# Two-of-eight experts: the bf16 division as a logarithm and an exponential, PSUM copies on VectorE, and the expert steps in a new order

## What is computed

```python
scores = jax.nn.sigmoid((xt @ gate.T).astype(jnp.float32))
_, sel = jax.lax.top_k(scores + expert_bias[None, :], TOP_K)      # TOP_K = 2 of 8
...
routed = (routed.astype(jnp.float32) * scores_sorted[:, None]).astype(x.dtype)
xb = routed.astype(jnp.bfloat16)
for e in range(NUM_EXPERTS):
    h = jax.nn.silu(xb @ w1e.T) * (xb @ w3e.T)                    # in bfloat16
    oe = (h @ w2e.T).astype(routed.dtype)
    out_r = out_r + jnp.where((expert_ids == e)[:, None], oe, 0.0)
hs = jax.nn.silu(xt @ shared_w1.T) * (xt @ shared_w3.T)           # in float32
out = hs @ shared_w2.T
out = out.at[token_idx].add(out_r)
```

## Time and profile before

| | us |
|---|---|
| median of three runs | 3227.81 |
| lowest and highest | 3227.55, 3230.34 |
| span of the profiled execution | 3223.9 |
| first statistics of the expert stage start at | 2554.28 |
| last add to x of the expert stage ends at | 2775.66 |

### The profile page before, as it was taken

The page is one execution under the profiler, slowest core; times in us unless marked ns, Lnnn a source line. Parts: engine busy times, 40 slices in busy tenths (PEclk is TensorE's granted clock), DMA queues, the critical chain, the costliest instruction groups (busy, mean ns, idle before and its releaser), DMA issues. The chain is left out here.

```text
span 3223.9 us, 65738 instructions
## 1 busy us (share of the span) xinstructions
PE 2916.0 (90%) x18443; PEld 2458.6 (76%) x18444; DVE 2173.0 (67%) x4391; ACT 2039.8 (63%) x5203; POOL 1594.7 (49%) x2073
## 2 busy tenths in 40 slices
PE   5887999799999999999999999999999966599495
PEld 4665888588888888888888888888888833388463
DVE  7994444476677676677776677676777589766332
ACT  5664666577777776777677677677777456565121
POOL 6993333455555555555555555555555243465201
PEclk9998999899999999999999999999999878799598
DMA  4335666611111110111111011011010200342512
GB/s 133 115 117 153 203 203 204 208 34 50 45 44 40 45 51 33 45 51 34 44 51 44 34 51 45 33 51 45 33 51 14 82 1 0 113 147 80 189 43 78
DMA packets 253268, 245.07 MB, mean 76 GB/s; under 512 B 11769, under 2 KB 233473, under 8 KB 252929
## 3 DMA queue, kind: packets, MB, share of 16 engines
q1 hardware_dynamic: 237248, 223.15, 21.2%
q10 hardware_dynamic: 14144, 13.63, 1.5%
q0 software_dynamic: 1536, 4.20, 0.4%
HBM read 151.03 MB, written 89.92 MB: 75 GB/s over the span
## 5 line engine op out<-in xcount | busy, mean ns | idle before, releaser
L977 DVE TENSOR_TENSOR pt_lo<-ps_t,pt_hi 128x512 fp32r<-128x512 f32 (+1 forms) x1024 | 656.8, 641 | 383.2 <-ACT pt_hi L882 347.7
L882 ACT ACTIVATE pt_hi<-ps_t 128x512 fp32r<-128x512 f32 (+1 forms) x1024 | 571.4, 558 | 453.6 <-PE ps_t L1108 418.5
L1035 POOL TENSOR_SCALAR prob<-prob,inv_sum 128x512 f32<-128x512 f32 (+2 forms) x1024 | 640.1, 646 | 193.2 <-DVE inv_sum L968 193.2
L952 DVE TENSOR_REDUCE piece_max<-ps_s 128x1 f32<-128x512 f32 (+2 forms) x1024 | 626.5, 622 | 158.1 <-PE ps_s L1096 134.2
L871 ACT ACTIVATE prob<-ps_s,neg_max 128x512 f32<-128x512 f32 (+2 forms) x1024 | 649.9, 635 | 73.9 <-DVE neg_max L959 65.9
L1108 PE MATMUL ps_t<-ident,prob 128*128 128x128 f32 x3712 | 573.6, 273 | 30.5 <-DVE pt_lo L977 30.5
L1127 PE MATMUL ps_o<-pt_hi,v_hi 128*128 128x256 f32 x1856 | 596.9, 322 | 0.0
L1108 PEld LDWEIGHTS ps_t<-ident,prob 128*128 128x128 f32 x3712 | 459.6, 141 | 103.9 <-DVE pt_lo L977 36.3
L1129 PE MATMUL ps_o<-pt_hi,v_lo 128*128 128x256 f32 x1856 | 523.4, 282 | 0.0
L1128 PE MATMUL ps_o<-pt_lo,v_hi 128*128 128x256 f32 x1856 | 522.5, 282 | 0.0
L1091 PE MATMUL ps_s<-k_hi,q_hi 128*128 128x512 f32 (+2 forms) x1024 | 399.5, 390 | 25.2 <-DVE k_lo L992 12.1
(11 more groups left out here) (234 smaller groups left out, 5458.9 us busy)
## 6 DMA issues: line engine op xcount, KB each, us to landing
v_scratch<-v_out SPq DMA_DIRECT2D x120, 256.0 KB, 2.5
raw_k<-k_scratch SPq DMA_DIRECT2D x32, 960.0 KB, 5.2
raw_v<-v_scratch SPq DMA_DIRECT2D x32, 960.0 KB, 4.7
k_scratch<-k_out SPq DMA_DIRECT2D x104, 256.0 KB, 2.6
q_scratch<-out_t SPq DMA_DIRECT2D x64, 256.0 KB, 2.6
raw_q<-q_scratch SPq DMA_DIRECT2D x32, 512.0 KB, 3.4
c_raw<-in_ctx_t ACTq DMA_DIRECT2D x52, 256.0 KB, 2.8
raw_t<-in_ctx_t SPq DMA_DIRECT2D x24, 512.0 KB, 4.1
```

Of the source, the lines that this page charges most:

```text
L882: nc.scalar.activation(pt_hi[:, k % RING, cols], ps_t[:, k % 2, cols], ACT.Copy).then_inc(hi_done, 1)
L952: nc.vector.tensor_reduce(piece_max[:, n % 2, p:p + 1], ps_s[:, p, lo - p * PC:hi - p * PC], AX.X, ALU.max).then_inc(max_ready, 1)
L977: nc.vector.tensor_tensor(pt_lo[:, k % RING, cols], ps_t[:, k % 2, cols], pt_hi[:, k % RING, cols].bitcast(F32), ALU.subtract).then_inc(lo ...
L1035: nc.gpsimd.tensor_scalar(prob[:, n % PB, lo:hi], prob[:, n % PB, lo:hi], inv_sum[:, n % PB:n % PB + 1], 1.0, ALU.mult, ALU.mult).then_inc ...
```

## The change

It does six things, all in `moe_two_of_eight`:

1. The experts' `inv` is no longer a reciprocal on VectorE. ScalarE takes the logarithm of `den` into the fp32 tile `log_den` and then exp(-log_den). The shared expert keeps its fp32 reciprocal. A table that holds both functions is loaded at the start of the stage.
2. VectorE, not ScalarE, copies `h1` out of PSUM, with a floor of -44 under it, and copies both halves of `y` for steps 1 to 7. ScalarE keeps `h3`, `xbt` and the last step's two halves.
3. PSUM is cut anew: two banks of `h1`, one of `h3`, two of `y` (one for each half). The shared expert's `h3` is now copied by ScalarE, its `h1` stays in the bank that step 2 needs.
4. `xn` and `weight` are made once for all 16 tiles, ahead of the groups; `prepare` and `xr` are gone. GpSimd casts all weights first.
5. On TensorE the sums of a step come one step later, ahead of the next outputs, both halves together.
6. The shared expert's reciprocal stands behind VectorE's copy of step 1's `h1`.

The core of the diff:

```diff
-        xn = sb("xn4", [P, GT, D])
-        xr = sb("xr4", [P, 4, D])
+        xn = sb("xn4", [P, NT, D])
+        log_den = sb("log_den4", [P, N])
-        ps_h = psum("ps_h4", [P, 4, 512])
+        ps_h1 = psum("ps_h1_4", [P, 2, 512])
+        ps_h3 = psum("ps_h3_4", [P, 512])
-        ps_y = psum("ps_y4", [P, 512])
+        ps_y = psum("ps_y4", [P, 2, 512])
...
             def _(act):
+                nc.scalar.preload_act_table_set("natural_log_exp_and_others")
...
+                def inverse(i, s):
+                    j = s % 2
+                    act.wait_ge(den_ready, i * E0 + s)
...
+                    nc.scalar.activation(log_den[:, :], den_bf[:, j, :], ACT.Ln).then_inc(log_ready, 1)
+                    act.wait_ge(log_ready, i * E0 + s)
...
+                    nc.scalar.activation(inv_bf[:, j, :], log_den[:, :], ACT.Exp, scale=-1.0).then_inc(inv_ready, 1)
...
+                def copy_h1(i, s):
+                    j = s % 2
+                    dve.wait_ge(h1_ready, i * STEPS + s + 1)
...
+                    nc.vector.tensor_scalar(h1_bf[:, j, :], ps_h1[:, j, :], EXP_FLOOR, None, ALU.max).then_inc(h1_copied, 1)
...
+                def outputs(i, s, h):
+                    k = (i * E0 + s - 1) * 2 + h
+                    dve.wait_ge(y_done, k + 1)
...
+                    nc.vector.tensor_copy(y_bf[:, h, :], ps_y[:, h, :]).then_inc(y_copied, 1)
...
                 def group(i, last):
...
+                    copy_h1(i, 1)
+                    shared_inverse(i)
+                    denominator(i, 1)
+                    shared_gated(i)
+                    if positive(i):
+                        add_x(i - 1)
+                    for s in range(1, STEPS):
+                        if s >= 2:
+                            outputs(i, s - 1, 0)
+                        if s < LASTS:
+                            copy_h1(i, s + 1)
+                        if s >= 2:
+                            outputs(i, s - 1, 1)
+                        gated(i, s)
+                        if s < LASTS:
                             denominator(i, s + 1)
                         elif not last:
                             denominator(i + 1, 0)
...
+                def hidden(i, s):
...
+                        pe.wait_ge(xbt_copied, i * E0 + s)
+                        if s == 2:
+                            pe.wait_ge(siluf_ready, i + 1)
```

More of the change, by code:

```diff
@@ L1352, in _ @@
+                inputs(0, 0)
+                exponential(0, 0)
+                copy_h3(0, 0)
                 group(0, False)
@@ L1387, in choose @@
                     dve.wait_ge(chosen_s, 1)
+                    nc.vector.tensor_tensor(weight[:, :, :], chosen[:, :, :], score[:, :, :], ALU.mult).then_inc(weighted, 1)
                 def add_x(i):
@@ L1405, in places @@
-                def places(s):
-                    j = s % 2
-                    if s == 0:
-                        return exp_f[:, :], den_f[:, :], inv_f[:, :], silu_f[:, :], act_f[:, :], ps_h[:, 0, :], ps_h[:, 1, :]
-                    return exp_bf[:, j, :], den_bf[:, j, :], inv_bf[:, j, :], silu_bf[:, j, :], act_bf[:, j, :], h1_bf[:, j, :], h3_bf[:, j, :]
-                def denominator(i, s):
-                    exp, den = places(s)[:2]
-                    dve.wait_ge(exp_ready, i * STEPS + s + 1)
-                    nc.vector.tensor_scalar(den, exp, 1.0, None, ALU.add).then_inc(den_ready, 1)
@@ new lines, in add, with shared_outputs @@
+                def add(t, a, b, first=False, last=False):
+                    return nc.tensor.matmul(ps_acc[:, t // 2, (t % 2) * D:(t % 2) * D + D], a, b, start=first and t % 2 == 0,
+                                            stop=last and t % 2 == 1, skip_group_check=True)
+                def shared_outputs(i):
+                    pe.wait_ge(act_ready, i * STEPS + 1)
+                    if positive(i):
+                        pe.wait_ge(x_added, i * 2)
+                    for t in range(GT):
+                        last = add(t, act_f[:, t * P:t * P + P], sw[:, 2, :], first=True)
+                    last.then_inc(shared_done, 1)
@@ new lines, in outputs @@
+                def outputs(i, s, h):
+                    if h == 0:
+                        pe.wait_ge(act_ready, i * STEPS + s + 1)
+                    if s >= 2:
+                        pe.wait_ge(y_copied, i * 2 * (LASTS - 1) + (s - 2) * 2 + h + 1)
+                    elif positive(i):
+                        pe.wait_ge(y_last_copied, (i - 1) * 2 + h + 1)
+                    for t in range(2):
+                        last = nc.tensor.matmul(ps_y[:, h, t * D:t * D + D], act_bf[:, s % 2, (2 * h + t) * P:(2 * h + t + 1) * P], w_bf[:, 2, s - 1, :],
+                                                start=True, stop=True)
+                    last.then_inc(y_done, 1)
@@ L1556, in group @@
                         elif not last:
-                            hidden(0, i + 1)
-                        if s > 1:
-                            sums(s - 1, 1)
+                            hidden(i + 1, 0)
+                        if s + 1 < E0:
+                            inputs(i, s + 1)
+                        elif s == LASTS and not last:
+                            inputs(i + 1, 0)
+                        if s >= 2:
+                            sums(i, s - 1, 0)
+                            sums(i, s - 1, 1)
@@ L1572, in group @@
-                    if last:
-                        sums(STEPS - 1, 1)
+                            sums(i - 1, LASTS, 0)
+                            sums(i - 1, LASTS, 1)
+                        if s:
+                            outputs(i, s, 0)
+                            outputs(i, s, 1)
                 pe.wait_ge(gate_loaded, 32)
```

320 lines of the change are left out of this document (155 added, 165 removed).

## The result

The changed kernel took 3188.52 us in the median of four runs (3186.98 to 3190.98), the kernel before 3227.68 beside it (3225.28 to 3230.34): a ratio of 0.9881 with a 95% interval of 0.9867 to 0.9895. Forecast were 3193.4, in a range of 3183 to 3208. The span of the profiled execution is 3185.2 us, 38.7 less than before.

The account below looks back on a forecast made before the run. VectorE, with 32 bf16 reciprocals (107 of its 190 busy us), was taken as the bound. Stage end 2599.9 + 24 x 3.6 + 3 x 16.2 + 6.4 = 2741.3 against 2775.66, 34.4 us less: 3193.4 us, range 3183 to 3208.

Parts of the forecast that it names:

- the round trip worked out: Expert step: from act through TensorE's outputs, VectorE's three copies and silu back to act; 3.6 us, 3.36 if GpSimd doesn't matter.
- this neighbour: GpSimd's scaling beside VectorE's silu, act and denominator in nearly every step; 0.24 us added per step.
- the hole: VectorE's 0.64 us between act and copying y half 0, filled only by the next denominator; 0.1 to 0.4 idle expected.
- ScalarE's cover: In the step, the next denominator ends 0.58 us after act; ScalarE delays over 0.06 us would delay the step.
- The crossing: From the seventh expert's act through last and shared experts to the next group's first act: 16.2 us, against 16.85 before.
- a chosen mixture: At the crossing, TensorE between full and half clock after long idle: first outputs ready 1.2 us behind act.
- Start and tail: Stage's ends: first outputs at 2599.9, no gain at the start; 6.4 us from the last seventh act to the end.
- The level of TensorE: Rival: clock still swings between full and half within steps; step 3.9 us, 7.2 us more, 3200.6 us; chance 0.12.
- The half level throughout: Rival: TensorE stays at 1.2 GHz through the stage and becomes the bound; steps 4.6, 3236.7 us; chance 0.03.
- the table loads: Rival: ScalarE reloads tables at each function change, 2 x 1.283 us per step; steps 5.8, 3246 us; chance 0.01.
- The step of 4.23 us: Step length from which TensorE at 1.2 GHz throughout the stage was said to decide.
- A net change of zero: Rival: chained waits from ScalarE's missing slack stretch the step to about 4.7 us, no net change; chance 0.03.

Follow-up runs that it names:

- GpSimd quiet: Changed kernel with GpSimd scaling only 16 of 256 columns after the first two scalings: 3183.59 us, 0.9869 of the kernel before.
- the filler: Changed kernel with 14 extra matmuls on TensorE, results unread, ahead of expert 2's hidden rows at each crossing: 3184.59 us, 0.9874.
- the second profile: Changed kernel, nothing altered, timed and profiled again on another variant's chip (also the second set of runs): 3189.43 us, 0.9891.

## Why the prediction was right, and where it was off

**The bound and what replaces it.** Right. The reciprocals went, and the step became the round trip worked out. On its parts: a copy was to take 0.60 from start to start and takes 0.60 (2641.39 to 2641.99); the logarithm 0.63 in the sum (about 0.60 among the signs) and takes 0.630; the way from the end of `act` to the copy of `y` half 0 was to take 0.64 and takes 0.57 in the middle groups (2640.21 to 2640.78), 0.49 in the outer ones. That the step is this trip and not VectorE's sum was only argued; the run without the denominator shows it.

**GpSimd.** I had estimated 0.24 us from one row of 0.61 against 0.42; `silu` and `act` together lose 0.30. Step forecast 3.6, measured 3.55: the stretch was 0.06 too small, the rest of the trip 0.11 too long (3.36 instead of 3.25), and that they nearly cancel is luck. I had let every step have this neighbour. The last step of a group has none (3.22 to 3.25), nor have the last three of the last group (3.31, 3.22, 3.15), and in the first step of that group only `act` is hit (3.37), so 24 steps took 83.1 us, not 86.4. This is the largest error within the stage, 3.3 us: 1.2 from the size of the step, 2.1 from the steps without a neighbour.

**VectorE idle in the hole.** Wrong as a sign to look for. I wrote that 0.1 to 0.4 us would be idle ahead of `y` half 0. None is beside GpSimd, since the denominator too is stretched, to 0.45, and fills the hole; only the last copies of each group have 0.28 to 0.38 idle ahead of them. Who had looked for the bound by idle time alone would have named VectorE.

**ScalarE's cover.** Right in size. I had the next denominator end 0.58 us behind `act` in a hole of 0.64; it ends 0.49 behind it (2640.70) in one of 0.57. The exponential ends at 2640.22, just as `act` does. ScalarE's own round has more room: with GpSimd quiet it is full at 3.25, in a step of 3.55 it waits the other 0.30 for the denominator and the transposes. Where the run without a denominator has steps without GpSimd's stretch they take 3.21 to 3.25, so the trip and ScalarE's round can't be told apart there.

**The crossing.** The sum was 16.2, measured 16.69, 16.64 and 16.41. Its chain holds almost row by row: from the end of `act` of expert 7, reciprocal done at 10.6 (10.7 to 10.8 measured), `silu_f` at 11.5 (11.5 to 11.6), add to x at 13.3 (13.4 to 13.7), `act` at 15.0 (15.0 to 15.4). The outputs were to come 1.2 us behind `act`, a chosen mixture between the full level and half; they start 1.29 to 1.60 behind it (2635.23 to 2636.73 in the first crossing). That the filler saves 1.16 to 1.25 is another quantity, and its likeness to the 1.2 is chance. Two things I missed: `den_f` took 0.66 to 0.74 instead of 0.43, and I let the shared outputs follow `silu_f` directly, though in two of three crossings they wait for the add to x. Forecast crossings 48.6 in all, measured 49.7.

**Start and tail.** First outputs were forecast 45.6 us behind the stage's first statistics; they start 46.1 behind them (2599.18), and their copy 46.5 (47.3 in the second profile). The forecast's last part, 4.7 us from `silu_f` to the outputs, doesn't come out of what it is said to: 3.05 us of work with three quarters of the time at half level are 4.9, with three quarters of the work 5.3. Measured are 4.9 (2594.27 to 2599.18). The tail from the last seventh `act` was to take 6.4 and takes 5.9 (2731.91 to 2737.83).

**Sum.** The stage was to go from 221.4 to 187.0 and went to 184.75 (185.55 in the second profile). The forecast of 34.4 us saved thus became 36.6 in the stage (steps 3.3 less than forecast, crossings 1.1 more, start 0.5 more, tail 0.5 less) and 38.7 in the span; the 2.1 us between them lie in stages that the change doesn't touch. In the second set of runs the difference of medians was 35.0. The distance of forecast and median, 4.9 us, is 2.2 in the stage, 2.1 outside it, and 0.6 because the median lies 3.3 us above the span and not 3.9. That the errors within the stage cancel in part is luck.

**Rivals.** The level of TensorE doesn't swing in the steps (1.00), though in each it idles 0.70 us ahead of the outputs and 0.32 ahead of the second pair of sums. The section on PSUM-queue depth-cycling in the Trainium skill ("TensorE: Matmul & The Clock Gate"), which I weighed against this, has no counterpart here in steps of 3.55 us; in the run with the reciprocal on VectorE, with steps near 7 us, the clock is 0.67. The half level throughout and the table loads didn't come: the stage's only load stands ahead of all its steps. The step of 4.23 us, from which TensorE at half level was said to decide, has no working; twice its 2.16 us are 4.32. A net change of zero wasn't near.

## What to carry to other kernels

When a long operation leaves the bounding engine, don't divide work by engines for the new step, but follow one value once around all of them: the trip gave 3.36 us plus its neighbour's cost, where the sums of the engines gave 2.9, 3.2 and 2.16. Then test the answer by taking work away from the engine that looks full; if a hole opens and the step stays, that engine is not it. And look at the seams between loops first of all: putting the shared expert's exponential and act ahead of work with later users gave another 11 us, more than any run here gained within the steps (5.2 us, with GpSimd quiet), and kept TensorE at its upper level besides.

## What the runs showed of the hardware

- Beside GpSimd's scaling, bf16 operations of VectorE on SBUF tiles stretch: `silu` 0.41 to 0.55 or 0.59, `act` 0.42 to 0.58, `den_bf` 0.29 to 0.45 us; its fp32 reciprocal doesn't (3335 to 3344 ns). GpSimd's four scalings go from 1.84 to 2.19 beside the first three, and stay at 1.84 beside the reciprocal.
- A division as logarithm and exponential on ScalarE takes two instructions of 0.630 us for 128x512, with no table load between them; the reciprocal on VectorE takes 3.34 in bf16 as in fp32.
- Fourteen bf16 matmuls whose results nobody reads, in an idle time of 3.39 us, shortened the crossing by 1.2 us, since the eight fp32 matmuls behind them took 1.99 instead of 3.23 us.
- A scaling of 16 columns on GpSimd takes 0.36 us (four in 1.43), one of 256 columns 0.46 (four in 1.84): most of the time doesn't depend on the columns. Beside the short ones `silu` and `act` still keep their 0.41 and 0.42.
- In steps of 3.55 us with idle pieces of 0.70 and 0.32 TensorE keeps a granted clock of 1.00. Behind 3.39 us of idle time it was 0.76 in 2631.0 to 2634.4 and 0.68 in 2634.4 to 2637.2; behind 3.17 us in the last crossing of the run with short scalings it stayed at 1.00.
